# Cross attention with two heads side by side in the array's rows, a ring of keys and values, and part of the sums on ScalarE

## What is computed

```
q = (text_embeds @ Wq.T + bq).reshape(num_texts, num_words, HEADS, HEAD_DIM)
k = (video_embeds @ Wk.T + bk).reshape(num_vids, num_frames, HEADS, HEAD_DIM)
v = (video_embeds @ Wv.T + bv).reshape(num_vids, num_frames, HEADS, HEAD_DIM)
logits = jnp.einsum('avhd,bthd->abhvt', k, q) / math.sqrt(HEAD_DIM)
weights = jax.nn.softmax(logits, axis=3)
attn = jnp.einsum('avhd,abhvt->abhtd', v, weights)
attn = attn.reshape(num_vids, num_texts, num_words, EMBED)
attn = attn.mean(axis=0)
return attn @ Wo.T + bo
```

## Time and profile before

| | us |
|---|---|
| median of three runs | 2643.03 |
| the profiled execution's own time | 2661.52 |
| its span, first to last instruction | 2659.7 |
| of it, cross attention between 670 and 2268 us | 1598 |
| TensorE busy in the span | 2223.3 |
| VectorE, ScalarE, GpSimd busy | 2017.1, 1757.2, 1522.3 |

### The profile page before, as it was taken

The page is one execution under the profiler, slowest core; times in us unless marked ns, Lnnn a source line. Parts: engine busy times, 40 slices in busy tenths (PEclk is TensorE's granted clock), DMA queues, the critical chain, the costliest instruction groups (busy, mean ns, idle before and its releaser), DMA issues. The chain is left out here.

```text
span 2659.7 us, 48294 instructions
## 1 busy us (share of the span) xinstructions
PE 2223.3 (84%) x12615; PEld 1588.4 (60%) x12616; DVE 2017.1 (76%) x3304; ACT 1757.2 (66%) x4921; POOL 1522.3 (57%) x1668
## 2 busy tenths in 40 slices
PE   4605688673899999999999999999999999767773
PEld 2304577563566666666666666666666666656663
DVE  5806775304799999999999999999999999565554
ACT  2205321352788888888888888888888888225552
POOL 2241342363577777777777777677677677325552
PEclk9757665796899999999999999999999999769997
DMA  6311103111000000000000000000000000311114
GB/s 217 116 39 48 48 25 95 42 42 46 1 0 0 1 0 0 0 0 0 0 0 0 0 0 0 0 0 0 0 0 0 0 0 0 103 36 36 36 36 113
DMA packets 70362, 71.94 MB, mean 27 GB/s; under 512 B 21376, under 2 KB 55296, under 8 KB 70272
## 3 DMA queue, kind: packets, MB, share of 16 engines
q1 hardware_dynamic: 51696, 49.44, 6.4%
q0 software_dynamic: 8192, 16.87, 2.4%
q10 hardware_dynamic: 10384, 4.66, 0.6%
HBM read 53.07 MB, written 17.87 MB: 27 GB/s over the span
## 5 line engine op out<-in xcount | busy, mean ns | idle before, releaser
L1835 POOL TENSOR_TENSOR attend_weights<-attend_weights,attend_scales 128x512 f32<-128x512 f32 x1024 | 1048.3, 1046 | 477.3 <-DVE attend_scales L1751 477.3
L1729 DVE TENSOR_REDUCE attend_maxima<-attend_psL 128x16 fp32r<-128x1024 f32 x512 | 623.8, 1218 | 88.4 <-PE attend_psL L1651 88.4
L1745 DVE TENSOR_REDUCE attend_sums<-attend_weights 128x16 f32<-128x1024 f32 x512 | 618.6, 1208 | 4.3 <-ACT attend_weights L1781 4.1
L1795 ACT ACTIVATE attend_turned<-attend_psT 128x512 f32<-128x512 f32 x1024 | 557.1, 600 | 9.9 <-PE attend_psT L1670 6.6
L1670 PE MATMUL attend_psT<-consts,attend_weights 128*128 128x128 f32 x4096 | 531.2, 272 | 1.1 <-POOL attend_weights L1835 0.9
L1670 PEld LDWEIGHTS attend_psT<-consts,attend_weights 128*128 128x128 f32 x4096 | 477.0, 140 | 70.9 <-POOL attend_weights L1835 3.0
L1683 PE MATMUL attend_psA<-attend_turned,attend_chunk_values 128*64 128x512 f32 x2048 | 495.9, 605 | 0.8 <-ACT attend_turned L1795 0.8
L1789 ACT ACTIVATE attend_weights<-attend_psL,attend_maxima 128x64 f32<-128x64 f32 x2048 | 448.7, 334 | 51.1 <-DVE attend_maxima L1729 51.1
L1650 PE MATMUL attend_psL<-keys,attend_q_high 128*128 (+1 forms) x1024 | 435.3, 425 | 7.1 <-ACT attend_weights L1789 5.5
L1651 PE MATMUL attend_psL<-keys,attend_q_low 128*128 (+1 forms) x1024 | 404.9, 395 | 0.0
L1781 ACT ACTIVATE attend_weights<-attend_psL 128x512 f32<-128x512 f32 x512 | 315.8, 617 | 0.6 <-PE attend_psL L1660 0.6
(11 more groups left out here) (326 smaller groups left out, 2688.3 us busy)
## 6 DMA issues: line engine op xcount, KB each, us to landing
select_xbuf<-in_x_dram SPq DMA_DIRECT2D x16, 1024.0 KB
select_emb<-L_attn_video_embeds_dram ACTq DMA_DIRECT2D x16, 256.0 KB, 3.0
values_gates<-project_vg SPq DMA_DIRECT2D x8, 512.0 KB, 2.6
retain_vg<-values_gates SPq DMA_DIRECT2D x8, 512.0 KB, 3.5
moe2back_back<-result SPq DMA_DIRECT2D x8, 512.0 KB, 7.3
normed<-moe2route_normed SPq DMA_DIRECT2D x4, 520.0 KB, 8.9
moe_w<-in_L_ffn_W_dram SPq DMA_DIRECT2D x1, 2048.0 KB, 10.8
normed<-moe1route_normed SPq DMA_DIRECT2D x4, 512.0 KB, 5.1
```

The costliest lines, as they stand in the source:

```text
L1729: dve.tensor_reduce(maxima[:, both, :].rearrange("p j v -> p (j v)"), psL[:, both, :].rearrange("p j (v f) -> p (j v) f", f=FR), X, ALU.ma ...
L1745: dve.tensor_reduce(sums[:, both, :].rearrange("p j v -> p (j v)"), weights[:, both, :].rearrange("p j (v f) -> p (j v) f", f=FR), X, ALU. ...
L1795: act.activation(turned[:, parity, :, j * P:(j + 1) * P], psT[:, j % 2, :].rearrange("p (k q) -> p k q", k=SUB), ACT.Copy).then_inc(turned ...
L1835: pool.tensor_tensor(w, w, scales[:, s, :, None].to_broadcast([P, VC, FR]), ALU.mult).then_inc(normalised, 1)
```

## The change

**Keys and logits.** `keys` now holds head 0 in partitions 0 to 63 and head 1 in partitions 64 to 127, high parts in its first half of columns and low parts in the second. A pair of units is the same row tile for both heads. Its logits are three products (q_high k_high, q_high k_low, q_low k_high; the product of the low parts is dropped), each a matmul over 64 rows for each head: six matmuls of 64 rows where there were four of 128. A step is two row tiles, both heads, and one chunk; a run is one batch, 32 steps.

**Ring.** SyncE copies each chunk's keys (512 KB) and values (256 KB) by DMA from where they lie into a ring of two slots; the copy on GpSimd is gone. A chunk serves two steps. Each mix is eight matmuls of 256 columns instead of four of 512.

**Sums.** For the first four videos of unit 0, `accum_out` of the exponential gives the sum; VectorE's sum over the first pair is 768 elements wide instead of 1024.

**Around it.** One key matmul, one high part and one low part (128 partitions) for each chunk in the selection; eight runs with eight projections instead of sixteen; four steps in the rolled part instead of two. Crossout reads `mixedT` directly, by 64-row matmuls for the two heads, without the staging copy.

```diff
-                    def logits(n, h, key, j):
-
-                        pe.wait_ge(exped, 4 * n + (j + 1))
-                        tile = slice(j * P, (j + 1) * P)
-                        pe.matmul(psL[:, j, :], q_high[h][:, tile], K.keys[:, ds(key, KC)], start=True, stop=False, skip_group_check=True)
-                        pe.matmul(psL[:, j, :], q_low[h][:, tile], K.keys[:, ds(key, KC)], start=False, stop=(SHIFTED_BY[j] != "TensorE"),
-                                  skip_group_check=True).then_inc(logits_ready, 1)
+                    def logits(n, p, k, pair):
+
+                        units = (2 * pair, 2 * pair + 1)
+                        pe.wait_ge(exped, 4 * n + (units[1] + 1))
+                        products = ((q_high, 0), (q_high, 1), (q_low, 0))
+                        for x, (q, part) in enumerate(products):
+                            for j in units:
+                                h, t = unit(j)
+                                tile = slice((k % 2 * 2 + t) * P, (k % 2 * 2 + t + 1) * P)
+                                last = x == len(products) - 1
+                                mm = pe.matmul(psL[:, j, :], q[p][head_rows(h), tile], key_ring[head_rows(h), k // 2, part, :],
+                                               start=(x == 0), stop=(last and SHIFTED_BY[j] != "TensorE"), skip_group_check=True)
...
-                        for k in range(SUB):
-                            part = slice((k % 2) * DH1, (k % 2 + 1) * DH1)
-                            mm = pe.matmul(psA[part, :], chunk_values[:, parity, k, :], turned[:, parity, k, :],
-                                           start=(first and k < 2), stop=(k >= SUB - 2), skip_group_check=True)
+                        for t in range(SUB):
+                            for h in range(H1):
+                                mm = pe.matmul(psA[head_rows(h), r * 2 * P:(r + 1) * 2 * P], value_ring[:, slot, h, t, :],
+                                               turned[:, parity, t, h].rearrange("p t l -> p (t l)"),
...
+                    def load(slot, c, uses):
+
+                        if uses is not None:
+                            sp.wait_ge(logits_ready, uses * 8)
+                        sp.dma_start(key_ring[:, slot].bitcast(F32), keys[:, :, ds(c * KC, KC)].bitcast(F32)).then_inc(keys_in[slot], 16)
+                        if uses is not None:
+                            sp.wait_ge(chunks_mixed, uses * 2)
+                        sp.dma_start(value_ring[:, slot].rearrange("p h t e -> p h (t e)"),
+                                     K.values[:, :, ds(c * SUB, SUB), :].rearrange("p h t e -> p h (t e)")).then_inc(values_in[slot], 16)
...
-                                    ins = act.activation(into[:, video], psL[:, j, video], ACT.Exp, bias=maxima[:, j, v:v + 1].bitcast(F32))
+                                    own = sums[:, 4 * parity + j, v:v + 1] if v < SUMMED else None
+                                    ins = act.activation(into[:, video], psL[:, j, video], ACT.Exp, bias=maxima[:, j, v:v + 1].bitcast(F32), accum_out=own)
...
-                    def keep_values(n, parity, h, c):
-                        pool.tensor_copy(chunk_values[:, parity, :, :], K.values[:, h, ds(c * SUB, SUB), :]).then_inc(values_set, 1)
```

More of the change, by code:

```diff
@@ L383, in _ @@
                 act.wait_ge(weightT_ready, 5)
[L384 to L389, removed]
+                act.activation(K.wq[:], psT[:, 0, 0:D], ACT.Copy, scale=LOGIT_SCALE).then_inc(weightT_copied, 1)
+                act.activation(wkT[:], psT[:, 0, D:2 * D], ACT.Copy).then_inc(weightT_copied, 1)
                 act.activation(wvT[:], psT[:, 0, 2 * D:3 * D], ACT.Copy).then_inc(weightT_copied, 1)
@@ L399, in chunk @@
                         load(c + 4, s)
[L400 to L403, removed]
+                    act.wait_ge(keys_ready, c + 1)
+                    act.activation(K.keys[:, ds(c * KC, KC)], psK[:, s % 2, :], ACT.Identity, bias=bk[:, 0:1]).then_inc(key_highs, 1)
                 with act.Fori(0, TURNS - 1) as it:
@@ L1593, in cross_attention @@
             turned_ready, turned_copied = sem("turned_ready"), sem("turned_copied")
[L1594 to L1600, removed]
+            chunks_mixed, run_copied = sem("chunks_mixed"), sem("run_copied")
@@ L1602, in place, with unit, per_step @@
+            def unit(j):
+                return j % H1, j // H1
             def place(j):
                 return shifted_on[SHIFTED_BY[j]].index(j) + 1
-            def per_chunk(j):
+            def per_step(j):
                 return len(shifted_on[SHIFTED_BY[j]])
             def steps_of(engine, step):
[L1613 to L1626, removed]
@@ L1628, in index, with run @@
-            def index(b, h, c):
-                return (b * H1 + h) * NKC + c
+                def run(i, p):
+                    for s in range(FIRST):
+                        step(i, p, s, s % 4, s // 4)
+                    with engine.Fori(0, (STEPS - FIRST) // 4) as it:
+                        for k in range(4):
+                            step(i, p, it * 4 + (FIRST + k), k, it + FIRST // 4)
+                for p in range(2):
+                    run(0, p)
+                with engine.Fori(1, B // 2) as i:
+                    for p in range(2):
+                        run(i, p)
@@ L1632, in exists, with index, quarter @@
+                for s in range(LAG):
+                    step(B // 2, 0, s, s % 4, s // 4)
+            def index(i, p, s):
+                return (i * 2 + p) * STEPS + s
+            def quarter(i, p, q):
+                return (i * 2 + p) * (STEPS // 4) + q
             def exists(n):
-                return not isinstance(n, int) or 0 <= n < CHUNKS
+                return not isinstance(n, int) or 0 <= n < B * STEPS
             def videos(ap):
@@ L1821, in step @@
                         if exists(n) and early == 1:
[L1822 removed]
+                            high(1 - p, i * 2 + p + 2)
                     act.nop().then_inc(run_copied, 1)
```

235 lines of the change are left out of this document (116 added, 119 removed).

## The result

| | before | after |
|---|---|---|
| median, us | 2641.69 (2639.49 to 2645.39, 4 runs) | 2692.53 (2688.49 to 2695.7, 4 runs) |
| after / before | | 1.019 (95%: 1.017 to 1.021) |
| profiled execution, us | 2661.5 | 2690.44 |
| a step of the attention, us | 6.11 | 6.40 |

The change makes the kernel 50.8 us slower; the forecast was 2684, 41 us slower.

What follows compares the result with a forecast made beforehand. TensorE was taken to bound the attention step: -0.46 + 0.74, say +0.27 us over 256 steps, is +69; with +1 - 7 - 4 - 12 - 6 that is +41 us, forecast 2684 us, range 2545 to 2712.

Steps and rivals of the forecast that it cites:

- TensorE sets the step; nothing else reaches it: Cross attention: TensorE needs 6.11 us a step before and 6.39 after; the chains of VectorE and ScalarE stay below it.
- -0.46 from three rounds of two: Attention logits: a pair takes three rounds of two simultaneous 64-row matmuls instead of four matmuls, -0.46 us a step.
- rival of no overlap: Attention logits: the two heads' matmuls run in turn, +1.67 us a step, 3043 us in all; chance 0.04.
- +0.74 for four changes of shape: Attention step: four more switches between 64-row and 128-row matmuls on TensorE, 0.15 to 0.20 us each, +0.74 us together.
- rival of cheap changes: Attention step: switching to and from 64-row matmuls costs little, so the kernel takes 2497 to 2635 us; chance 0.33.
- Sums: 0 to 0.21 each, hidden: Attention: four ScalarE exponentials with a second output cost 0 to 0.21 us each, VectorE saves 0.27; both under TensorE, worth 0.
- rival of dear sums: Attention: ScalarE's sums cost more than 0.21 us each; at 0.3, 2753 us; chance 0.05.
- The sign named for it: Profile after: an extra, long ScalarE instruction behind each of four exponentials would show the prediction wrong.
- GpSimd and the ring: 0: Attention: GpSimd has slack and chunk loads land in 2.6 us, some 6 us being available, so 0 a step.
- The +1 for the start: Start of the attention: waiting for the ring's first keys costs +1 us once.
- Runs -11, selection -12, crossout -6: Around attention steps: fewer projections -7 and loop turns -4, selection's fewer low parts -12, crossout's paired matmuls -6 us.
- likeliest case: Whole kernel: the forecast case, 2660 to 2708 us, with changes of shape at 0.66 to 0.80 us a step; chance 0.54.

Runs made afterwards that it cites:

- e2: Changed kernel with the dropped fourth product (q_low times k_low) put back as a 64-row matmul for each head: 2760.51 us, 121 us more than the changed kernel.
- e5: Changed kernel with both units of a pair using head 0's queries and keys, so the same half of the rows: 3065.16 us, 354 more than the changed kernel.
- e1: Changed kernel with each pair's six 64-row logit matmuls replaced by three 128-row ones (logits not the reference's): 2509.44 us, 130 less than the changed kernel.
- e4: Changed kernel with the second logit group moved ahead of unit 1's shift, right behind the mix: 2593.04 us, 46 less than the changed kernel.
- e3: Changed kernel with all sums back on VectorE, none on ScalarE: 2635.0 us, 4 less than the changed kernel, step still 6.40 us.
- e6: Changed kernel with three 128-row logit matmuls for a pair and all sums on VectorE: 2569.04 us, 0.9658 of the kernel before, step 5.85 us.
- e7: Changed kernel with unit 1's shift moved from TensorE to VectorE and six sums of unit 0 on ScalarE: 2620.32 us, 0.9845 of the kernel before.
- e8: Kernel before with unit 1's shift moved from TensorE to VectorE and six sums of unit 0 on ScalarE: 2644.72 us, 0.9940 of the kernel before.

## Why the prediction was right

- **TensorE sets the step; nothing else reaches it.** Right. Its busy time, VectorE's longer wait and e2 (118 us expected of 512 rounds, 121 measured) show it.
- **-0.46 from three rounds of two.** Right. Pairs start together, e5 turns the overlap off and costs 354 us, and e2 puts 0.236 on a round. The rival of no overlap is out.
- **+0.74 for four changes of shape.** 0.77 by the timeline, 0.76 by e2 against the kernel before: 0.19 each, above the 0.14 at which the change would have broken even. The 32-row rows gave the right price for 64 rows: entering the logits 0.09 of late start and 0.12 of first load (0.20 forecast), leaving them 0.18 towards the shift and 0.15 towards transposes (0.19, 0.15 forecast). The rival of cheap changes, the strongest at 0.33, is out: e1 takes them away and saves 130 us, e4 takes one away and saves 46. Its 0.16 for one change is less than the average.
- **Sums: 0 to 0.21 each, hidden.** 0.09 each, and hidden (e3). The rival of dear sums is out for this kernel. The sign named for it did appear, an extra ScalarE instruction of 0.20 us behind each of four exponentials; its length was no measure of its price. Once TensorE is relieved, the sums are worth 0.05 us a step (e6).
- **GpSimd and the ring: 0.** No wait of 1400 to 1600 us names the arrival of keys or values; the keys land in 3.1 us while SyncE's queue waits up to 14 us for a slot. The +1 for the start didn't show: no wait of 630 to 680 us names the ring either.
- **Runs -11, selection -12, crossout -6.** Measured -8.5, -11 and -6.3. The term of the projections was right (eight times 0.85); the -4 for the turns of the loop was not, they gave about -1. The prediction counted passes and took each turn to cost the same, but a turn of the changed kernel is nearly three times as long.
- **The sum.** Forecast +41, measured +50.8: 6.5 us from a step that is 0.296 and not 0.27 longer, 2.5 from the runs, 1 from the selection, less the 1 of the start; the last 1 is the difference between the sum above, 49.7, and the medians. The result lies in the range 2660 to 2708 that was given to the likeliest case.

What stays open: why a change costs 0.09 of late start. The traces show that it does, at every change of the step and for every pair of shapes there, not what the array does in it.

## What to carry to other kernels

Packing two heads side by side saved a round here only because a product was dropped; with all four products (e2) the rounds are as many as with full rows. The price is paid for each change of shape, 0.16 to 0.19 us, or some three quarters of a round of 512 columns here. So by an estimate from these prices a packed group between full-row work has to save some one and a half rounds to pay, and this one saved one. That longer packed stretches pay follows from the same prices, but no run here has one. Before packing, count the changes in one turn of the loop, from the order of instructions, and try to put packed groups next to each other or next to work that is packed already, as e4 did. And a relief of an engine that waits (the sums here) is worth nothing until the bound moves; move the bound's own work to it, as e7 did. That move needs nothing of the change: e8 has it in the kernel before.

## What the runs showed of the hardware

- A change between 64-row and 128-row matmuls costs what one between 32-row and 128-row ones does, and one between 128 columns and 64: 0.15 to 0.21 us at the full clock, as 0.09 of late start and 0.05 to 0.12 of a weight load that is no longer hidden.
- Two 64-row matmuls of 512 columns in fp32r on different halves of the rows take one round of 0.232 us; on the same half they take two.
- A sum taken along with an exponential of 64 columns is an ACTIVATION_READ_ACCUMULATOR of its own, 0.20 us long in the trace of the kernel after, that adds only 0.09 to the time from one exponential to the next.
- Loads of 512 and 256 KB for the ring, 61 GB/s, stood beside four busy engines without a visible cost: a maximum over 1024 elements took 1.218 us on average before and 1.220 after.
